# VectorE's comparison and its second take of token numbers change places within a group of four tiles

## What is computed

```
idx_flat = topk_idx.reshape(-1)
sort = jnp.argsort(idx_flat)
tok = sort // TOPK
x_sorted = x_flat[tok]
g = jax.lax.ragged_dot(x_sorted, we_gate, group_sizes)
u = jax.lax.ragged_dot(x_sorted, we_up, group_sizes)
o = jax.lax.ragged_dot(jax.nn.silu(g) * u, we_down, group_sizes)
y = jnp.zeros_like(x_flat).at[tok].add(o * w_sorted[:, None])
```

## Time and profile before

| | |
|---|---|
| median of 3 runs | 4031.53 us (4031.32 to 4032.81) |
| profiled execution | 4030.18 us |
| its span | 4028.5 us |
| TensorE, matmuls | busy 91% |
| VectorE | busy 58% |
| ACT | busy 33% |
| GpSimd | busy 41% |
| the expert stage | from about 906 us to the end |

### The profile page before, as it was taken

The page is one execution under the profiler, slowest core; times in us unless marked ns, Lnnn a source line. Parts: engine busy times, 40 slices in busy tenths (PEclk is TensorE's granted clock), DMA queues, the critical chain, the costliest instruction groups (busy, mean ns, idle before and its releaser), DMA issues.

```text
span 4028.5 us, 108723 instructions
## 1 busy us (share of the span) xinstructions
PE 3672.8 (91%) x16856; PEld 2818.4 (70%) x16857; DVE 2318.3 (58%) x5815; ACT 1312.3 (33%) x4031; POOL 1642.9 (41%) x1208
## 2 busy tenths in 40 slices
PE   6719999959999999999999999999999999999996
PEld 3304444537778777787878777787888778778785
DVE  5364555555565655656655565556555566556553
ACT  2212222213333333334333333333333343333331
POOL 1010000004555555555555454555555555545443
PEclk9959999979999999999999999999999999999998
DMA  3422323225666666667666665666666677666654
GB/s 111 108 68 83 96 91 100 91 52 131 139 133 151 150 148 121 149 124 177 125 131 126 158 133 118 136 139 148 124 125 141 118 165 160 129 126 155 129 102 76
DMA packets 216834, 502.39 MB, mean 125 GB/s; under 512 B 47244, under 2 KB 47372, under 8 KB 216018
## 3 DMA queue, kind: packets, MB, share of 16 engines
q0 software_dynamic: 129024, 320.94, 42.4%
q1 hardware_dynamic: 87250, 177.78, 13.5%
q10 hardware_dynamic: 512, 3.15, 0.4%
HBM read 1115.65 MB, written 191.41 MB: 324 GB/s over the span
## 4 chain that ended last, share of the span: by engine, by line
PE 60%; issue 5%; DVE 4%; DVEq 2%; DMA 2%; ACT 2%; ACTq 1%; SPq 0%; POOLq 0%; POOL 0%
PE e_ps_gu L1476 35%; PE e_ps_y L1495 16%; PE e_ps_x L1446 5%; DVE e_w_low L1617 3%; PE e_ps_h L1505 3%; DMA out<-e_y,e_y_ids 2%; PE e_ps_find L1458 2%; ACT e_w_high L1554 1%; DVEq L1330 1%; DVE e_past L1649 1%; ACTq L1330 0%; DVEq L1617 0%; DVE e_below L1660 0%; ACT e_silu L1573 0%; DMA e_w_raw<-in_L_ffn_we_down 0%
## 5 line engine op out<-in xcount | busy, mean ns | idle before, releaser
L1410 POOL DMA_INDIRECT out<-e_y,e_y_ids x576 | 978.6, 1699 | 1340.0 <-SPq L1380 551.4
L1402 POOL DMA_INDIRECT e_x<-token_rows,e_x_ids x576 | 614.1, 1066 | 276.2 <-issue 172.4
L1476 PE MATMUL e_ps_gu<-e_w_high,e_xT_high 128*128 x2304 | 695.2, 425 | 21.3 <-issue 12.7
L1476 PE MATMUL e_ps_gu<-e_w_low,e_xT_high 128*128 x2304 | 651.5, 406 | 0.3 <-issue 0.3
L1476 PE MATMUL e_ps_gu<-e_w_high,e_xT_low 128*128 x2304 | 644.9, 402 | 0.0
L1573 ACT ACTIVATE e_silu<-e_ps_gu 128x256 f32<-128x256 f32 x576 | 221.7, 385 | 1128.3 <-PE e_ps_gu L1476 1096.3
L1644 DVE TENSOR_SCALAR e_y<-e_ps_y,e_weight 128x512 f32 (+1 forms) x576 | 430.7, 748 | 266.0 <-PE e_ps_y L1495 254.4
L1625 DVE TENSOR_TENSOR e_xT_low<-e_ps_x,e_xT_high 128x512 fp32r<-128x512 f32 x576 | 397.7, 690 | 279.2 <-ACT e_xT_high L1562 187.9
L1476 PEld LDWEIGHTS e_ps_gu<-e_w_low,e_xT_high 128*128 128x128 f32 x2304 | 443.8, 193 | 111.1 <-issue 5.3
L1476 PEld LDWEIGHTS e_ps_gu<-e_w_high,e_xT_low 128*128 128x128 f32 x2304 | 443.3, 192 | 109.8
L1476 PEld LDWEIGHTS e_ps_gu<-e_w_high,e_xT_high 128*128 128x128 f32 x2304 | 403.6, 195 | 96.0 <-issue 33.1
(11 more groups left out here) (253 smaller groups left out, 3948.2 us busy)
## 6 DMA issues: line engine op xcount, KB each, us to landing
e_w_raw<-in_L_ffn_we_gate SPq DMA_DIRECT2D x576, 512.0 KB
e_w_raw<-in_L_ffn_we_up SPq DMA_DIRECT2D x576, 512.0 KB
e_w_raw<-in_L_ffn_we_down SPq DMA_DIRECT2D x576, 512.0 KB
a_x<-in_L_attn_x SPq DMA_DIRECT2D x64, 256.0 KB, 3.4
t_x_in<-in_L_attn_x SPq DMA_DIRECT2D x64, 256.0 KB, 2.8
token_rows<-t_xn SPq DMA_DIRECT2D x64, 256.0 KB, 3.1
out<-t_y_out SPq DMA_DIRECT2D x64, 256.0 KB, 2.0
e_x<-token_rows,e_x_ids POOLq DMA_INDIRECT x576
```

Source lines behind the costliest of these rows:

```text
L1402: pool.indirect_dma_start(x[:, s % XS, :], None, k.rows, bass.IndirectOffsetOnAxis(x_ids[:, s:s + 1], 0)) \
L1410: pool.indirect_dma_start(k.out, bass.IndirectOffsetOnAxis(y_ids[:, s:s + 1], 0), y[:, s % YS, :], None, compute_op=ALU.add).then_inc(adde ...
L1476: last = nc.tensor.matmul(ps_gu[s % 2][:], x[:, s % 2, c, :], w[:, c], start=(n == 0), stop=(n == 3 * DC - 1))
```

## The change

In VectorE's program the comparison of a quad moves from its third step to its second, and the second take of the quad before moves from the second to the third.

```diff
                 split_low(i, s, 1)
-                if s == 1 and exists(i - s - SHORT + AHEAD_FIND):
+                if s == 1 and exists(i - s + AHEAD_FIND):
+                    mark(i - s + AHEAD_FIND)
+                if s == 2 and exists(i - s - SHORT + AHEAD_FIND):
                     pick(i - s - SHORT + AHEAD_FIND, 2)
-                if s == 2 and exists(i - s + AHEAD_FIND):
-                    mark(i - s + AHEAD_FIND)
                 if s == 3 and exists(i - s + AHEAD_FIND):
                     pick(i - s + AHEAD_FIND, 0)
                 hidden(i, s)
```

## The result

The changed kernel takes 4026.14 us, the median of 20 runs, against 4034.03 us for the kernel before, also of 20 (the three times shown ahead of the change are among them). The ratio is 0.998 with an interval of 0.9973 to 0.9988: faster by 0.2%, where 0.5% slower was forecast. The profiled execution took 4020.54 us, its span is 4018.8 us, 9.7 us less than before. I take the account from these two traces.

The account below looks back on a forecast made before the run. TensorE, busy 91% of the span, was taken as the bound, so late VectorE signals cost only what it can't fill. 7.7 + 2.0 - 2 + 10.8 = 18.5 us gave 4050 us, range 4038 to 4060.

Parts of the forecast that it names:

- D and its floor: From VectorE finishing `past` to TensorE's `gate_up`: 2.47 us undisturbed, floor 1.70 to 1.80; lateness costs only from there.
- undisturbed quads: D falls from 2.47 to 1.94 us at no cost; fifteen with late table loads pay, +2.0 us in all.
- New weights at the fourth tile alone: In 14 quads the whole delay of `find`'s signal lands on TensorE: 0.55 us each, 7.7 us, clock apart.
- the clock term: TensorE behind `find`: ten waits, lifted to 0.8 to 1.05 us, lose 1.08 us each at lower clock, 10.8 us.
- the ten short waits: Waits of `find` with new weights at the fourth tile, 0.29 to 0.51 us before the change, never losing clock.
- Already behind at the second step: 42 quads, new weights at first, second or third tile: VectorE passes on 0.63 us, pays back 0.53; -2 us.
- Rival 4: Faster: long waits for `past`, mostly third-tile, gain 0.1 us, two thirds keep the clock, 20 us back; 4021, chance 0.04.

Follow-up runs that it names:

- Run 7: The changed kernel with the comparison moved to the first step, the second take staying in the third: 4011.17 us, ratio 0.9955.
- experiments 2 and 3: Against the kernel before, comparison moved to the second step beside the take (3919.04 us), or to the first with the take in the second (3919.51 us).
- experiment 8: Against the kernel before, second take moved to the first step and comparison to the second, nothing in the third: 3933.75 us, ratio 0.9748.
- `early_loads`: The kernel before with its order kept, VectorE loading table words earlier, ahead of the comparison or take: 4133.12 us, ratio 1.0239.

## Why the prediction was wrong, step by step

- **D and its floor**: right. D measured from `tile_ids` is 1.95 us in the median of undisturbed quads (1.94 forecast), and 1.7 to 1.8 where VectorE is late, the floor of before. The take's end comes 0.53 us later than the comparison's would, as taken. Undisturbed quads cost 0.6 us instead of 2.0.
- **New weights at the fourth tile alone**: the place was right, and that the total agrees so well (18.9 and 18.5 us) is partly luck. The waits grew by 5.8 us in sum (7.7 forecast); the remaining 13.1 us are time at the lower granted clock (10.8 forecast, from four rows). From the start of `find` to SiLU, 13 of these quads take about 6 us instead of 4.57, against 4 before. Run 7 shows that the clock term could as well have been 6. One reading under it was wrong: the ten short waits were not all without a loss. The one of 0.51 us, at 1358 us, took 6.10 us from `find` to SiLU at a granted clock of 0.66, so nine quads were left to lose the clock, and all but one of them did.
- **Already behind at the second step**: this step failed. I wrote that `pick` holds VectorE for 1.87 us and `mark` for 1.24, that 0.63 us are passed on and 0.53 paid back. The 0.63 is right: in the third-tile quad `h` follows the start of `gate_up` by 0.86 us, and by 1.47 before. What I left out is the rest of the step. Behind `pick` the next table load shows (0.41 us in this quad, medians of 0.39 and 0.52 in the third-tile and first-tile quads), behind `mark` it doesn't (-0.07). So not 0.63 but 1.0 to 1.1 us are passed on, half a microsecond net per quad instead of 0.05, and this term of the sum is -32.5 us instead of -2. The sum priced that load at nothing in either order, and put nothing on GpSimd's gather because its order didn't change. But `pick` with its internal waits holds the load back into the gather, where it takes 0.75 to 0.89 us instead of 0.30; with `mark` it is over before the gather begins. The numbers stood in the trace: I had put the gap down as given, "VectorE's table loads come late", without asking what went before it and what ran beside it.
- What half a microsecond buys was then missed too. At the third tile the waits shrank by 10.6 us in sum (36.5 to 25.9) for -21.9 us; the other 11 came from the clock, for 12 of the 18 quads fell to the lower one behind `find`, and 17 before. At the first tile no wait was listed at all, only a restart at the floor, and 0.6 us each came back, so that `find` takes 0.40 us again instead of 0.9.
- **Rival 4** (faster through the clock at the third tile) had the place right, and that a shorter wait lets some quads keep the clock. But it gave these waits 0.1 us where they lost 0.55, and left out the first tile. The account is 18.9 + 0.6 - 32.5 + 3.4 = -9.6 us: two effects of about 20 and 30 us against each other. That the sum is so near zero is chance.
- **What neither order removes**: both signals behind new weights. An empty third step is worth 117 us, 2.9%, in experiments 2 and 3 (the kernel before took 4036.35 us beside them), and 2.5% in experiment 8.

## What to carry to other kernels

When two pieces of work change places on an engine, count for each not only its own span but the gap up to the next piece that follows. A wait for the engine's own results holds the sequencer, and the register loads behind it begin later. Then look at what the other engines do at that moment: here a load that began inside GpSimd's gather took 0.8 us instead of 0.3, and by the account above this decided the sign of the result. Then ask whether either piece must stand where a rare long job (here a split of weights every ninth tile) can get in front of it; moving both signals ahead of it was worth over ten times the swap. A net change near zero can be two large ones, and it is the table by kind of quad that shows them.

## What was not expected of the hardware

- A register load on VectorE (L1330) takes 0.31 us by itself and 0.85 us in the median where it begins inside a gather on GpSimd (84 of 702 loads in the kernel before). A load that begins 0.4 to 1.0 us behind the start of a gather of the usual 1 us ends about 1.4 us behind that start (median of 553 loads in the traces of all ten kernels).
- With the register steps around it, the load takes the sequencer about 0.7 us: placed where nothing covers it, the issue time ahead of `past` went from 0.63 to 1.35 us in `early_loads`.
- TensorE restarts slowly from a wait that sits on a register instruction: 1.70 to 1.80 us from the signal to the first matmul of `gate_up`, in many quads at a granted clock of 1.00, while the list of waits shows 0.3 us or nothing. In the quad of the earlier trace rows the sequencer's rows fill this time: the step with the wait at 1939.92, then one about every 0.1 us up to 1941.48, and `gate_up` at 1941.59.
- Waits of `find` of the same sum (13.3 and 13.0 us in the same 14 quads) went with 11.9 and 18.9 us of lost time. The clock's share of a wait is not a constant of its length.
